# Softmax attention on one Trainium2 core: the maxima's low parts, the projections' low halves and the output sums moved to in front of a quarter's fourth maximum

## The chip, the cores and the metric

The kernel runs on one core of a Trainium2 chip. The metric is the time of one execution on the device, in microseconds (us), taken as the median of several runs. Profiled executions give a trace of each engine: TensorE (PE, matrix products), VectorE (DVE), ScalarE (ACT), GpSimd (POOL), SyncE (SP, which issues DMAs). PEld is TensorE's loading of weights.

## The reference

Two blocks are computed one after the other: a layer norm, an attention, a mixture of eight experts, and a gated sum onto the input. Only the attention of the first block is touched by the change. It is an ordinary softmax attention over 8 sequences of 512 tokens, 128 features, 16 heads of 8 features:

```python
qkv = x @ w_qkv + b_qkv
q, k, v = ...                       # (8 sequences, 16 heads, 512 tokens, 8)
attn = jnp.einsum('bhqd,bhkd->bhqk', q, k) * hd ** (-0.5)
attn = jax.nn.softmax(attn, axis=-1)
out = jnp.einsum('bhqk,bhkd->bhqd', attn, v)
return out @ w_proj + b_proj
```

## The kernel before

Each engine has its own list of instructions, written out by hand in one function per engine (`attend`), and the engines wait for one another by semaphores. An engine works through its list in order.

**Steps and quarters.** The attention runs in steps u. Step u belongs to sequence b = u // 4 and to its group of four heads g = u % 4, so that 32 steps carry exponentials; a few steps before and after fill and drain the pipeline. Each step has four quarters t, and each quarter four heads j; i = 4t + j counts from 0 to 15. The i-th turn of step u does two products on TensorE: one of scores turned around (keys by queries, L1022, semaphore `st_mm`) for step u, whose exponentials ScalarE writes (L1297, `exp_set`), and one of scores (L1028, `s_mm`) for step u + 2, whose negated row maxima VectorE takes (L1667, `max_set`). The first kind is here called an exponential's product, the second a maximum's product, S0 to S15, and its maximum M0 to M15. The maxima are added into the product of the exponentials' scores two steps later, as two more rows of the queries: a high part and a low part.

**Banks.** There are eight banks of PSUM. The maxima's products use three banks in turn (0, 1, 7), the exponentials' products three others (2, 3, 4), the output products bank 5. So a product must wait until the one three places before it has been read; the function `read_before` holds these numbers, with one exception, the sixteenth product of a step, which takes the second bank.

**Bank 6.** Everything else goes through bank 6, one small job after another:

- end of quarter 0, every step: the transpose of the step's sixteen maxima (L1052, `nmT_mm`). ScalarE copies its high part (`m_hi`, L1315), VectorE subtracts for the low part (`m_lo`, L1682, `mlo_set`), and SyncE copies both into the queries' rows.
- end of quarter 1: the transposes of the output products (L1066, `oT_mm`), which wait for `mlo_set`. VectorE then takes reciprocals of the sums of exponentials (`rden`, L1691) and normalizes (L1693), behind M7.
- end of quarter 2 and of quarter 3 in steps with g = 2: the projections of keys and of queries for the sequence after next (`project`, L324 to L326). ScalarE writes their high halves, VectorE the low halves (`low_half`, L1656, `lo_set`). The second projection waits for the low half of the first, and the next step's transpose of the maxima (g = 3) waits for the low half of the second.
- end of quarter 3 in steps with g = 0: the product with the output weights (L1099, `out_mm`). VectorE adds the bias and writes the sequence's rows (L1698, `attn_set`). The next step's transpose of the maxima (g = 1) waits for `attn_set`.

**The third place of each quarter.** Within a quarter TensorE issues the output product of the quarter before (`output`, L1123, four wide products and their weights) behind turn j = 2. So the fourth product of each quarter comes about a microsecond behind the third.

**Before the change** VectorE does the second low half behind M0 (g = 3), the low part of the maxima behind M4, the first low half behind M12 (g = 2), and the output sums behind M15 (g = 0).

Of the kernel before, what the change touches and what calls it, by code (L numbers as in the profile page):

```python
# [21 lines left out]
F32 = mybir.dt.float32  # L22
# [4 lines left out]
ALU = mybir.AluOpType  # L27
# [3 lines left out]
P = 128  # L31
# [3 lines left out]
QT = SEQ // P  # L35
# [11 lines left out]
def build(nc, x, w_qkv, b_qkv, w_proj, b_proj, router_w, w1, v1, w2, ffn_bias,  # L47
          Wq, Wk, Wv, Wc, Ltri, Wr, br, Wi, bi, Wg, bg, Wo, bo, gamma, beta, out):
    D = x.shape[2]
# [19 lines left out]
    with ctx:  # L69
        def sb(name, shape, dt=F32):  # L70
            return ctx.enter_context(nc.sbuf_tensor(name, shape, dt))

        def sem(name):
            return ctx.enter_context(nc.semaphore(name))

        ps = ctx.enter_context(nc.psum_tensor("ps", [P, 8, 512], F32))
# [5 lines left out]
        attn = sb("attn", [P, TOK_TILES, D])  # L82
# [21 lines left out]
        bproj_bc = sb("bproj_bc", [P, D])  # L104
# [56 lines left out]
        m_hi = sb("m_hi", [16, 2, P], F32R)  # L161
        m_lo = sb("m_lo", [16, 2, P], F32R)
# [12 lines left out]
        def stage():  # L175
# [116 lines left out]
        s_mm, max_set, nmT_mm, mhi_set, mlo_set, m_in = (  # L292
            sem("s_mm"), sem("max_set"), sem("nmT_mm"), sem("mhi_set"), sem("mlo_set"), sem("m_in"))
# [6 lines left out]
        onT_mm, onT_set, out_mm, attn_set = sem("onT_mm"), sem("onT_set"), sem("out_mm"), sem("attn_set")  # L300
# [9 lines left out]
        def spread(ap, axis, shape):  # L310

            return ap.unsqueeze(axis).to_broadcast(shape)
# [5 lines left out]
        def rows_of(tile, b):  # L318

            return tile[:, b * QT:(b + 1) * QT, :] if isinstance(b, int) else tile[:, bass.ds(b * QT, QT), :]  # L320
# [64 lines left out]
        def bank_of(i):  # L385


            return 1 if i == 15 else i % 3
# [5 lines left out]
        def max_head(j):  # L394

            return (j + 2) % 4
# [1079 lines left out]
        def _(dve):  # L1476
# [119 lines left out]
            def choices_between(t, j):  # L1596

                if (t, j) == (0, 0):
                    sums(0)
                if (t, j) == (0, 3):  # L1600
                    first_candidates(0)
                    choice(0)
                if (t, j) == (1, 1):
                    first_out(0)
                if (t, j) == (1, 3):
                    second_candidates()
                if (t, j) == (2, 2):
                    choice(1)
                if (t, j) == (3, 1):
                    choice_weights(0)  # L1610

            def first_tiles():

                E3 = [P, EXPERTS, EXPERTS]
                link(dve.tensor_tensor(cmp8[:, :, :], spread(off[:, :], 2, E3), spread(thr[:, :], 1, E3), ALU.is_gt))
                link(dve.tensor_reduce(ntile[:, :], cmp8[:, :, :], AX, ALU.add))
                link(dve.tensor_tensor(cmp8[:, :, :], before8[:, :, :], spread(ntile[:, :], 1, E3), ALU.mult))
                link(dve.tensor_reduce(first[:, :], cmp8[:, :, :], AX, ALU.add))
                link(dve.tensor_scalar(off[:, :], first[:, :], float(TILE), None, ALU.mult))

            def tile_experts():

                N3 = [1, TILES, EXPERTS - 1]
                link(dve.tensor_tensor(ecmp[:, :, :], spread(first[0:1, 1:EXPERTS], 1, N3),
                                       spread(tile_no[:, :], 2, N3), ALU.is_le))
                return dve.tensor_reduce(eidf[:, :], ecmp[:, :, :], AX, ALU.add)
# [27 lines left out]
            def low_half(b, o, bank):  # L1654
                dve.wait_ge(hi_set, b * 2 + (o + 1))
                dve.scalar_tensor_tensor(Lo[:, 1 - o, :], ps[:, bank, :], cols[:, 1 - o:2 - o],  # L1656
                                         Hi[:, 1 - o, :].bitcast(F32), ALU.add, ALU.subtract).then_inc(lo_set, 1)

            def attend(u, g, b, now):
                gt, v = (g + 3) % GROUPS, u + 2  # L1660
                for t in range(4):
                    for j in range(4):
                        i = t * 4 + j
                        if now.max:
                            dve.wait_ge(s_mm, v * 16 + (i + 1))
                            at = max_head(j) * 4 + t
                            dve.tensor_reduce(nmax[:, g % 2, at:at + 1], ps[:, (0, 1, 7)[bank_of(i)], :], AX, ALU.max,  # L1667
                                              negate=True).then_inc(max_set, 1)
                        if isinstance(u, int) and u == -2:
                            choices_between(t, j)  # L1670
                        if isinstance(u, int) and u == -1 and (t, j) == (2, 1):
                            dve.wait_ge(e_set[0], 2)
                            first_tiles()
                            tile_experts().then_inc(hot_set[0], 1)
                        if (t, j) == (1, 0) and now.low:

                            dve.wait_ge(mhi_set, u + 2)
                            dve.wait_ge(nmT_mm, u + 2)
                            if not (isinstance(u, int) and u + 1 < 2):
                                dve.wait_ge(m_in, u * 32)  # L1680
                            r = (g + 1) % 2
                            dve.tensor_tensor(m_lo[:, r, :], ps[0:16, 6, 0:P], m_hi[:, r, :].bitcast(F32),  # L1682
                                              ALU.subtract).then_inc(mlo_set, 1)
                        if (t, j) == (0, 0) and now.halves:
                            low_half(b + 2, 1, 6)
                        if (t, j) == (3, 0) and now.next:
                            low_half(b + 2, 0, 6)
                        if (t, j) == (1, 3) and now.tail:
                            dve.wait_ge(oT_mm, u)
                            turned = ps[:, 6, :].rearrange("p (q j r) -> p q j r", q=QT, j=4)  # L1690
                            dve.reciprocal(rden[:, :, :], turned[:, :, :, HD]).then_inc(rden_set, 1)  # L1691
                            dve.wait_ge(rden_set, u)
                            dve.tensor_tensor(onorm[:, :, 32 * gt:32 * gt + 32].rearrange("p q (j r) -> p q j r", j=4),  # L1693
                                              turned[:, :, :, 0:HD], spread(rden[:, :, :], 3, [P, QT, 4, HD]),
                                              ALU.mult).then_inc(onorm_set, 1)
                        if (t, j) == (3, 3) and g == 0 and now.tail:
                            dve.wait_ge(out_mm, b)
                            dve.tensor_tensor(rows_of(attn, b - 1), ps[:, 6, :].rearrange("p (q d) -> p q d", q=QT),  # L1698
                                              spread(bproj_bc[:, :], 1, [P, QT, D]), ALU.add).then_inc(attn_set, 1)
# [221 lines left out]
            link(dve.tensor_scalar(fbias_bc[:, :], fbias_bc[:, :], 0.5, None, ALU.mult))  # L1921
            dve.sem_inc(attn_set, 1)
            steps(dve, attend)
            experts(0)
            block1_weights()
# [29 lines left out]
```

## Time and profile before

| | us |
|---|---|
| median of 3 runs | 1088.25 |
| fastest and slowest of them | 1087.11, 1091.65 |
| span of the profiled execution | 1101.2 |

| engine | busy in the span, us | share |
|---|---|---|
| TensorE | 980.5 | 89% |
| VectorE | 852.7 | 77% |
| ScalarE | 620.6 | 56% |
| GpSimd | 572.2 | 52% |

The trace begins with the first instruction and ends with the last, so the profiled execution's own time is its span. Matrix products are pipelined and the ends of their records are modelled: a busy TensorE is not TensorE at its peak. In the rows, a number in square brackets at the end is the time the engine sat idle before the instruction, with what ended it. A gap of a few hundredths is not shown. Steps can be told apart on VectorE by the low part of the maxima (L1682), one in each step: the one at 201.74 us is that of step 9 (g = 1), 212.88 of step 10, 225.97 of step 11, 249.32 of step 13.

### The profile page before, as it was taken

How to read it: one execution, taken by the hardware profiler on the slowest of the kernel's cores; microseconds unless marked ns; L12 is line 12 of the kernel's file. 1: busy time of each engine (PE TensorE's matmuls, PEld its weight loads, DVE VectorE, ACT ScalarE, POOL GpSimd, SP SyncE). 2: the span in 40 equal slices, each digit the busy share in tenths (PEclk: the TensorE clock that was granted, in tenths of full speed). 3: DMA queues.
4: the chain of work that ended last, by engine and by line, in shares of the span. 5: the costliest groups of instructions: out<-in, count | busy, mean ns of one | idle time of the engine just before them, and what ended most of it. 6: DMA issues, size and time to landing. Idle time of an engine off the chain costs nothing. (4 is left out here: it accounts for less than half of the span.)

```text
span 1101.2 us, 18065 instructions
## 1 busy us (share of the span) xinstructions
PE 980.5 (89%) x5608; PEld 634.8 (58%) x5608; DVE 852.7 (77%) x1910; ACT 620.6 (56%) x1248; POOL 572.2 (52%) x631
## 2 busy tenths in 40 slices
PE   5789999999999999989999964999996999999960
PEld 4542344343434344368888853756655888888850
DVE  7556899999979999435555548699992899999975
ACT  6115788888868888843333326333333666777642
POOL 7220687443435442015555556378782576777770
PEclk9995999999979999999999985699997999999985
DMA  6736566353535532216666635034312677687719
GB/s 209 300 104 193 160 193 209 101 169 113 170 101 170 178 116 88 87 58 195 207 197 187 205 95 146 20 108 126 93 44 82 180 214 208 208 224 220 218 56 236
DMA packets 121521, 170.37 MB, mean 155 GB/s; under 512 B 18801, under 2 KB 80594, under 8 KB 118354
## 3 DMA queue, kind: packets, MB, share of 16 engines
q1 hardware_dynamic: 94290, 110.94, 35.1%
q0 software_dynamic: 18688, 54.08, 14.3%
q10 hardware_dynamic: 8448, 4.20, 1.5%
q8 instruction: 45, 0.74, 0.3%
q14 instruction: 50, 0.41, 0.1%
HBM read 106.71 MB, written 63.76 MB: 155 GB/s over the span
## 5 line engine op out<-in xcount | busy, mean ns | idle before, releaser
L1667 DVE TENSOR_REDUCE nmax<-ps 128x1 f32<-128x512 f32 x512 | 324.8, 683 | 50.2 <-PE ps L1028 45.6
L1297 ACT ACTIVATE stage<-ps 128x512 f32<-128x512 f32 x512 | 274.4, 594 | 75.6 <-PE ps L1022 69.6
L841 POOL DMA_INDIRECT token_y<-stage,ids_now x184 | 182.7, 993 | 130.0 <-DVE stage L1723 58.3
L1028 PE MATMUL ps<-stage,stage 32*128 32x512 f32 x512 | 189.1, 521 | 14.1 <-DVE nmax L1667 12.8
L1022 PE MATMUL ps<-stage,stage 32*128 32x512 f32 x512 | 172.3, 496 | 9.0 <-ACT stage L1297 7.5
L797 POOL DMA_INDIRECT slots_x<-xn,pos x128 | 154.5, 1207 | 40.7 <-issue 39.6
L1168 PEld LDWEIGHTS ps<-stage,stage 128*128 128x128 f32 (+1 forms) x1288 | 164.9, 191 | 13.5 <-issue 1.8
L1168 PE MATMUL ps<-stage,stage 128*128 128x128 f32 (+1 forms) x1288 | 170.9, 275 | 1.5 <-issue 1.2
L1022 PEld LDWEIGHTS ps<-stage,stage 32*128 32x128 f32 x512 | 70.3, 188 | 158.0 <-ACT stage L1297 125.9
L324 PE MATMUL ps<-stage,stage 128*128 128x512 f32 x322 | 141.1, 438 | 3.6 <-issue 3.6
L1123 PE MATMUL ps<-stage,stage 128*32 128x512 f32 x1024 | 144.2, 637 | 0.0
L326 PE MATMUL ps<-stage,stage 128*128 128x512 f32 x322 | 127.8, 397 | 0.0
L325 PE MATMUL ps<-stage,stage 128*128 128x512 f32 x322 | 127.1, 395 | 0.0
L1350 ACT ACTIVATE stage<-ps 128x512 f32<-128x512 f32 (+1 forms) x69 | 41.2, 597 | 104.8 <-PE ps L326 83.0
L1028 PEld LDWEIGHTS ps<-stage,stage 32*128 32x128 f32 x512 | 75.6, 194 | 37.7 <-DVE nmax L1667 30.2
L1787 DVE TENSOR_TENSOR stage<-ps,stage 128x512 f32<-128x512 f32 (+1 forms) x69 | 47.5, 689 | 61.6 <-PE ps L326 36.9
L1352 ACT ACTIVATE stage<-ps,ebcol 128x512 f32<-128x512 f32 x92 | 63.2, 687 | 52.8 <-PE ps L326 24.1
L1791 DVE SCALAR_TENSOR_TENSOR stage<-stage,stage 128x512 f32<-128x512 f32 x92 | 71.3, 774 | 23.3 <-ACT stage L1355 16.9
L326 PEld LDWEIGHTS ps<-stage,stage 128*128 128x128 f32 x322 | 59.8, 186 | 15.6
L324 PEld LDWEIGHTS ps<-stage,stage 128*128 128x128 f32 x322 | 60.4, 188 | 11.9 <-issue 2.3
L325 PEld LDWEIGHTS ps<-stage,stage 128*128 128x128 f32 x322 | 60.4, 187 | 8.2
L1355 ACT ACTIVATE stage<-ps,ebcol 128x512 f32<-128x512 f32 x92 | 63.2, 687 | 0.6 <-PE ps L326 0.6
(226 smaller groups left out, 1537.4 us busy)
## 6 DMA issues: line engine op xcount, KB each, us to landing
stage<-halves_w SPq DMA_DIRECT2D x23, 1024.0 KB
stage<-halves_w SPq DMA_DIRECT2D x23, 704.0 KB
stage<-slots_x SPq DMA_DIRECT2D x46, 260.0 KB
stage<-q_halves SPq DMA_DIRECT2D x32, 256.0 KB
halves_w<-stage POOLq DMA_DIRECT2D x16, 512.0 KB
k_halves<-stage SPq DMA_DIRECT2D x24, 256.0 KB
q_halves<-stage SPq DMA_DIRECT2D x24, 256.0 KB
stage<-k_halves SPq DMA_DIRECT2D x128, 48.0 KB
```

The source lines that it names most:

```text
L324: pe.matmul(out_ap, w_hi_ap, x_hi_ap, start=start, stop=False)
L325: pe.matmul(out_ap, w_hi_ap, x_lo_ap, start=False, stop=False)
L326: return pe.matmul(out_ap, w_lo_ap, x_hi_ap, start=False, stop=stop)
L797: pool.indirect_dma_start(out=slots_x[L], out_offset=bass.IndirectOffsetOnAxis(ap=pos[:, c:c + 1], axis=0), in_=xn[:, t, :], in_offset=Non ...
L841: pool.indirect_dma_start(out=token_y, out_offset=bass.IndirectOffsetOnAxis(ap=ids_now[:, r, q:q + 1], axis=0), in_=ysb[:, r, q, :], in_of ...
L1022: pe.matmul(ps[:, 2 + bank_of(i), :], head_rows(Ks, g, j)[:, t * P:(t + 1) * P], head_rows(Qs, g, j), start=True, stop=True).then_inc(st_m ...
L1028: pe.matmul(ps[:, (0, 1, 7)[bank_of(i)], :], head_rows(Qs, g2, j2)[:, t * P:(t + 1) * P], head_rows(Ks, g2, j2), start=True, stop=True).th ...
L1123: mm = pe.matmul(ps[32 * j:32 * j + 32, 5, :], vaug[:, even, t, 4 * g + j, :], probs[:, t % 2, j, :], start=(t == 0), stop=(t == 3))
L1168: mm = pe.matmul(ps[:, 5 + r, q * P:(q + 1) * P], hT[0:M, par, q * P:(q + 1) * P], wdn[0:M, r, f, :], start=(f == 0 and q == 0), stop=(f = ...
L1297: act.activation(probs[:, t % 2, j, :], ps[:, 2 + bank_of(i), :], ACT.Exp, scale=SCALE).then_inc(exp_set, 1)
L1667: dve.tensor_reduce(nmax[:, g % 2, at:at + 1], ps[:, (0, 1, 7)[bank_of(i)], :], AX, ALU.max, negate=True).then_inc(max_set, 1)
L1791: dve.scalar_tensor_tensor(hT[:, par, :], gsig[:, par, :], 1.0, gact[:, par, :], ALU.add, ALU.mult).then_inc(h_set[L], 1)
```

## The change

Four instructions of VectorE's list move. No instruction is added, removed or altered, and the lists of the other engines stay as they are, with all their waits. The second low half moves from behind M0 to in front of M3, the low part of the maxima from behind M4 to in front of M7, the first low half from behind M12 to in front of M15, and the output sums from behind M15 to in front of M3 of the next step (those of the last sequence stay where they are).

```diff
                 for t in range(4):
                     for j in range(4):
                         i = t * 4 + j
+                        if (t, j) == (0, 3) and now.halves:
+                            low_half(b + 2, 1, 6)
+                        if (t, j) == (0, 3) and g == 1 and u > 1:
+                            dve.wait_ge(out_mm, b)
+                            dve.tensor_tensor(rows_of(attn, b - 1), ps[:, 6, :].rearrange("p (q d) -> p q d", q=QT),
+                                              spread(bproj_bc[:, :], 1, [P, QT, D]), ALU.add).then_inc(attn_set, 1)
+                        if (t, j) == (1, 3) and now.low:
+                            dve.wait_ge(mhi_set, u + 2)
+                            dve.wait_ge(nmT_mm, u + 2)
...
+                            dve.tensor_tensor(m_lo[:, r, :], ps[0:16, 6, 0:P], m_hi[:, r, :].bitcast(F32),
+                                              ALU.subtract).then_inc(mlo_set, 1)
+                        if (t, j) == (3, 3) and now.next:
+                            low_half(b + 2, 0, 6)
                         if now.max:
                             dve.wait_ge(s_mm, v * 16 + (i + 1))
...
-                        if (t, j) == (1, 0) and now.low:
...
-                        if (t, j) == (0, 0) and now.halves:
-                            low_half(b + 2, 1, 6)
-                        if (t, j) == (3, 0) and now.next:
-                            low_half(b + 2, 0, 6)
...
-                        if (t, j) == (3, 3) and g == 0 and now.tail:
+                        if (t, j) == (3, 3) and u == 32:
                             dve.wait_ge(out_mm, b)
```

VectorE's list before, from the normalizing of a step with g = 2 to that of the next one; the low halves write `stage_10`, the normalizing writes `stage_4`, and `nmax` takes the maxima:

```order
L1693 TENSOR_TENSOR stage_4<-ps,rden 128x4x32
L1667 TENSOR_REDUCE nmax<-ps 128x1 x5
L1656 SCALAR_TENSOR_TENSOR stage_10<-ps,cols,stage_9 128x512
L1667 TENSOR_REDUCE nmax<-ps 128x1 x4
L1656 SCALAR_TENSOR_TENSOR stage_10<-ps,cols,stage_9 128x512
L1667 TENSOR_REDUCE nmax<-ps 128x1 x4
L1682 TENSOR_TENSOR m_lo<-ps,m_hi 16x128
L1667 TENSOR_REDUCE nmax<-ps 128x1 x3
L1691 RECIPROCAL rden<-ps 128x16
```

The same place in VectorE's list after the change (line numbers are those of the changed kernel):

```order
L1698 TENSOR_TENSOR stage_4<-ps,rden 128x4x32
L1685 TENSOR_REDUCE nmax<-ps 128x1 x7
L1656 SCALAR_TENSOR_TENSOR stage_10<-ps,cols,stage_9 128x512
L1685 TENSOR_REDUCE nmax<-ps 128x1 x4
L1656 SCALAR_TENSOR_TENSOR stage_10<-ps,cols,stage_9 128x512
L1685 TENSOR_REDUCE nmax<-ps 128x1 x4
L1678 TENSOR_TENSOR m_lo<-ps,m_hi 16x128
L1685 TENSOR_REDUCE nmax<-ps 128x1
L1696 RECIPROCAL rden<-ps 128x16
```

Seven maxima now precede the first low half (M8 to M14), and only one stands between the low part of the maxima and the reciprocals.

VectorE's list before, around the end of a step with g = 0, where `attn` takes the output sums:

```order
L1693 TENSOR_TENSOR stage_4<-ps,rden 128x4x32
L1667 TENSOR_REDUCE nmax<-ps 128x1 x8
L1698 TENSOR_TENSOR attn<-ps,bproj_bc 128x512
L1667 TENSOR_REDUCE nmax<-ps 128x1 x5
L1682 TENSOR_TENSOR m_lo<-ps,m_hi 16x128
```

The same place after:

```order
L1698 TENSOR_TENSOR stage_4<-ps,rden 128x4x32
L1685 TENSOR_REDUCE nmax<-ps 128x1 x11
L1669 TENSOR_TENSOR attn<-ps,bproj_bc 128x512
L1685 TENSOR_REDUCE nmax<-ps 128x1 x4
L1678 TENSOR_TENSOR m_lo<-ps,m_hi 16x128
```

Three maxima of the next step now precede the output sums.

TensorE's list around the same place of steps 2 and 3 mod 4, which is the same in both kernels: the second projection (L324 to L326), three turns, the output product (L1123), the fourth turn, and the transpose of the maxima (L1052). What each waits for stands behind it:

```order
L1028 MATMUL ps<-stage_12,stage_13 128x512 [waits max_set]
L324 MATMUL ps<-xT_hi,wq_hi 128x512 [waits lo_set]
...
L1123 MATMUL ps<-stage_1,stage_11 32x512 [waits exp_set]
L1123 MATMUL ps<-stage_1,stage_11 32x512 x3
L1022 MATMUL ps<-stage_13,stage_12 128x512 [waits exp_set]
L1028 MATMUL ps<-stage_12,stage_13 128x512 [waits max_set]
L1052 MATMUL ps<-ident,nmax 16x128 [waits lo_set,max_set]
L1022 MATMUL ps<-stage_13,stage_12 128x512 [waits exp_set]
```

Nothing moved there; the instruction that ends two of these waits (`lo_set`) did.

## Rows read from the trace of the kernel before

**Rows 1.** The page's costliest group: busy us, mean ns, idle before, what ended it.

```profile
L1667 DVE TENSOR_REDUCE nmax<-ps 128x1 f32<-128x512 f32 x512 | 324.8, 683 | 50.2 <-PE ps L1028 45.6
```

**Rows 2.** Windows: length, busy per engine PE PEld DVE ACT POOL, clock, DMA.

```profile
220.00:240.00 20.00, 19.46 (x124) 8.18 (x123) 18.31 (x34) 16.29 (x33) 6.79 (x10) 1.00 0.59 181
```

**Rows 3.** VectorE's timeline, steps 9 to 11: start, length, line, count, idle before.

```profile
201.74 0.27 DVE L1682 TENSOR_TENSOR m_lo<-ps,m_hi 16x128 fp32r<-16x128 f32 x1
...
203.88 0.25 DVE L1691 RECIPROCAL rden<-ps 128x16 f32<-128x16 f32 x1
...
218.44 0.69 DVE L1667 TENSOR_REDUCE nmax<-ps 128x1 f32<-128x512 f32 x1 [0.48 <-PE ps L1028]
219.04 0.74 DVE L1656 SCALAR_TENSOR_TENSOR stage<-ps,cols,stage 128x512 fp32r<-128x512 f32 x1
219.70 1.96 DVE L1667 TENSOR_REDUCE nmax<-ps 128x1 f32<-128x512 f32 x3
222.32 0.69 DVE L1667 TENSOR_REDUCE nmax<-ps 128x1 f32<-128x512 f32 x1 [0.66 <-PE ps L1028]
222.93 0.74 DVE L1656 SCALAR_TENSOR_TENSOR stage<-ps,cols,stage 128x512 fp32r<-128x512 f32 x1
223.59 2.48 DVE L1667 TENSOR_REDUCE nmax<-ps 128x1 f32<-128x512 f32 x4
225.97 0.27 DVE L1682 TENSOR_TENSOR m_lo<-ps,m_hi 16x128 fp32r<-16x128 f32 x1
...
228.12 0.25 DVE L1691 RECIPROCAL rden<-ps 128x16 f32<-128x16 f32 x1
```

**Rows 4.** TensorE's timeline, steps 9 to 11.

```profile
203.13 0.66 PE L1066 MATMUL ps<-ident,stage 128*128 128x128 f32 x4
...
220.44 0.50 PE L1028 MATMUL ps<-stage,stage 32*128 32x512 f32 x1 [0.25 <-DVE nmax L1667]
220.86 0.50 PE L324 MATMUL ps<-xT_hi,wq_hi 128*128 128x512 f32 x1
...
221.76 0.49 PE L1028 MATMUL ps<-stage,stage 32*128 32x512 f32 x1
...
223.84 0.28 PE L1052 MATMUL ps<-ident,nmax 128*16 128x128 f32 x1
224.04 0.50 PE L1022 MATMUL ps<-stage,stage 32*128 32x512 f32 x1
```

**Rows 5.** VectorE's timeline, end of step 12 and first half of step 13.

```profile
245.73 0.69 DVE L1698 TENSOR_TENSOR attn<-ps,bproj_bc 128x512 f32<-128x512 f32 x1 [0.40 <-PE ps L1099]
246.34 3.07 DVE L1667 TENSOR_REDUCE nmax<-ps 128x1 f32<-128x512 f32 x5
249.32 0.27 DVE L1682 TENSOR_TENSOR m_lo<-ps,m_hi 16x128 fp32r<-16x128 f32 x1
...
251.46 0.25 DVE L1691 RECIPROCAL rden<-ps 128x16 f32<-128x16 f32 x1
```

**Rows 6.** TensorE's timeline, first quarter of step 13.

```profile
245.62 0.49 PE L1028 MATMUL ps<-stage,stage 32*128 32x512 f32 x1
...
247.70 0.28 PE L1052 MATMUL ps<-ident,nmax 128*16 128x128 f32 x1
```

**Rows 7.** ScalarE's timeline, step 11, the exponential of turn 7.

```profile
227.48 0.60 ACT L1297 ACTIVATE stage<-ps 128x512 f32<-128x512 f32 x1 [0.88 <-PE ps L1022]
```

**Rows 8.** A window at low clock; timelines of VectorE and TensorE around it.

```profile
310.00:320.00 10.00, 10.00 (x47) 3.26 (x39) 6.01 (x12) 4.95 (x10) 3.25 (x5) 0.58 0.22 80
...
296.87 0.27 DVE L1682 TENSOR_TENSOR m_lo<-ps,m_hi 16x128 fp32r<-16x128 f32 x1
...
304.63 0.68 PE L1022 MATMUL ps<-stage,stage 32*128 32x512 f32 x1 [0.67 <-ACT stage L1297]
...
308.21 0.69 DVE L1667 TENSOR_REDUCE nmax<-ps 128x1 f32<-128x512 f32 x1 [1.34 <-PE ps L1028]
...
326.67 0.27 DVE L1682 TENSOR_TENSOR m_lo<-ps,m_hi 16x128 fp32r<-16x128 f32 x1
```

More of the change, by code:

```diff
@@ L1663, in attend @@
                         i = t * 4 + j
+                        if (t, j) == (0, 3) and now.halves:
[7 more added lines that the diff above has]
+                            dve.wait_ge(nmT_mm, u + 2)
+                            if not (isinstance(u, int) and u + 1 < 2):
+                                dve.wait_ge(m_in, u * 32)
+                            r = (g + 1) % 2
+                            dve.tensor_tensor(m_lo[:, r, :], ps[0:16, 6, 0:P], m_hi[:, r, :].bitcast(F32),
+                                              ALU.subtract).then_inc(mlo_set, 1)
+                        if (t, j) == (3, 3) and now.next:
+                            low_half(b + 2, 0, 6)
                         if now.max:
@@ L1674, in attend @@
                             tile_experts().then_inc(hot_set[0], 1)
-                        if (t, j) == (1, 0) and now.low:
[L1677 to L1683, printed above, removed]
-                        if (t, j) == (0, 0) and now.halves:
-                            low_half(b + 2, 1, 6)
-                        if (t, j) == (3, 0) and now.next:
-                            low_half(b + 2, 0, 6)
                         if (t, j) == (1, 3) and now.tail:
```

## The prediction

> **What bounds the kernel now.** I read the groups on the page first [rows 1]. The 512 maxima (L1667) are the costliest group: 683 ns each, 324.8 us in all. The windows of the attention stage come next [rows 2]: from 220 to 240 us VectorE is busy 18.31 of 20 us, TensorE is shown busy 19.46 and ScalarE 16.29, at full clock. The three work in a ring: TensorE writes a score product, VectorE takes its maximum or ScalarE its exponential, and that frees the bank for the product three places on. So I do not cost by busy shares, I follow the ring. The timelines of VectorE [rows 3, 5] and TensorE [rows 4, 6] show it. Four maxima back to back take 2.48 us [rows 3], so one follows another after (2.48 - 0.68) / 3 = 0.60 us. VectorE's gaps are short and stand where TensorE has just done a block of other work. Every step therefore has this test: does the moved instruction fill such a gap, or does it make TensorE wait for what it used to have already?
>
> The stage repeats with a period of four steps. From the low part of the maxima in step 9 (201.74 us) to that in step 11 (225.97) is 24.23 us [rows 3]. I write M0 to M15 for a step's maxima, S0 to S15 for the products that feed them. S(i) needs M(i-3), except that S15 needs M13.
>
> **No instruction is added or removed.** Cost: nothing in busy time. The whole effect is in waits on bank 6, which carries one small job after another on TensorE, each waiting for the reader of the one before. TensorE takes its list in order: in [rows 4] S15 waits until 220.44 for M13, and the projection behind it, which needs nothing of M13, goes only at 220.86. So a job of bank 6 that waits also holds every product behind it.
>
> **Low half, fourth quarter (steps 2 mod 4).** Before: M12 218.44, low half 219.04 to 219.78, M13 219.70 [rows 3]; S15 waits for M13, the projection goes at 220.86 and S0 of the next step at 221.76, M0 at 222.32 [rows 3, 4]. After: M13 at 219.04, M14 at 219.64, low half at 220.25, done 0.74 later at 220.99. S15 no longer waits, but the projection does, for the low half: with the 0.06 us that a release takes here (M13 ends at 219.70 + 0.68 = 220.38, S15 starts at 220.44 [rows 3, 4]) it goes at 221.05. That is +0.19 us, in place of the wait of 0.25 us that goes. The gap before M15 is filled and the next wait is later by more.
>
> **Low half, first quarter (steps 3 mod 4).** Before: it starts at 222.93, straight behind M0, and is done at 223.67; the maxima's transpose, which waits for it, goes at 223.84, with S4 0.2 us behind it [rows 3, 4]. After, counted from M0 at the shifted 222.51: M1 223.11, M2 223.71, low half 224.31 to 225.05, transpose at 225.11, S4 0.2 later at 225.31 and, at about 0.5 us for a product with its drain and 0.06 for the release, M4 at 225.87. M3 runs meanwhile, from 224.97. Before, M4 started at 223.59 + 3 x 0.60 = 225.39 [rows 3]. So TensorE's transpose is late by 1.27 and VectorE by 0.48, since 0.8 of it were slack.
>
> **Low part of the maxima, every step.** Before, it starts at 201.74 (step 9) and TensorE's transposes of the output sums, which wait for it, go at 203.13 with time to spare [rows 3, 4]. After, two maxima later: 201.74 + 1.20 = 202.94, done at 203.21, the transposes at 203.27, +0.14. They take 0.66 [rows 4], so the reciprocal that waits for them starts at 202.94 + 0.27 + 0.06 + 0.66 + 0.06 = 203.99 against 203.88 [rows 3]: +0.11. In a step that is already late the same chain of 1.05 us from the start of the low part is the binding one. In step 11: M4 at 225.87, low part at 227.67, reciprocal at 228.72, against 228.12 [rows 3]: +0.60, and +0.63 on TensorE, 0.19 of it from the quarter before. The steps with nothing else get +0.15.
>
> **Output sums (moved from the end of steps 0 mod 4 to the next step).** Before: 0.40 us idle, then 245.73 to 246.42, M0 at 246.34, M4 four maxima later at 248.74, the maxima's transpose at 247.70, low part 249.32, reciprocal 251.46 [rows 5, 6]. After: the idle time is longer, not shorter, as M0 must wait for S0, which starts at 245.62 [rows 6] and so lets M0 go at 246.18. Then M1 246.78, M2 247.38, output sums 247.98 to 248.67, transpose 248.73 (+1.03), S4 248.93, M4 249.49 (+0.75), low part 251.29, its chain of 1.05 to the reciprocal at 252.34: +0.88. I take 0.90.
>
> ScalarE does not bind in any of these: its high part of the maxima is late with the transpose, but four exponentials on it sits idle for 0.88 us [rows 7], which covers the 0.5 that VectorE is late. SyncE's copy of the maxima's rows starts 1.2 us later; TensorE wants them only with the next step, about 6 us on, and no row of TensorE names a DMA: nothing. While the clock is low VectorE waits 1.34 us before the fourth maximum anyway [rows 8], which hides what now stands there: nothing. In the steps before the first exponentials one low half of each kind moves too; nothing in the rows prices them but the two terms above, so I bound them by 0.19 and 0.44 on either side and take 0. From M15 of step 29 on there are no maxima and nothing moves.
>
> **The sum.** At full clock: fourth quarter 6 x 0.19 = 1.1; first quarter 6 x 0.44 = 2.6 (0.63 less the 0.19 counted); output sums 7 x 0.90 = 6.3; plain low parts 13 x 0.15 = 2.0. Together 12.0 us. The bounds: each TensorE wait in full (1.27, 1.03, 0.19, 0.14) adds up to 7.6 + 7.2 + 1.1 + 1.8 = 18, and if VectorE alone counted and later gaps took it back, 0. I take 12, since all three engines shift by about the same and the later gaps (0.48 before M12, for one) are TensorE's work standing in front, so they shift too. The profiled execution, with 1101.2 us, is 1.2% above the median of 1088.25; the stage's pattern in it is regular, so I add the 12 to the median: 1100.3 us, and to the span: 1113.
>
> **Rivals.**
> A. *The waits don't bind and the gaps are filled (faster).* Each moved instruction stands where VectorE waits for the product behind TensorE's output product. If TensorE came to its transposes later than VectorE is through, the gain would be the gap of 0.66 before M0 [rows 3] six times and the 0.40 before the output sums [rows 5] seven times: 4.0 + 2.8 = 6.8, giving 1081.5. It decides itself at one point: the transpose must come over 1.27 us later than now, behind the low half. The rows put TensorE there before that [rows 4, 6]. Chance 0.09.
> B. *The lateness is taken back.* The gaps of VectorE that these rows show, 0.48, 0.66 and 0.40 [rows 3, 5], make 1.5 us in a period, against the 1.8 that a period loses (0.19 + 0.44 + 0.90 + 2 x 0.15). If they are slack rather than TensorE's own work, the time stays within 3 us of 1088. For: a wait that I place may fall on time that the ring had free through ScalarE. Against: S12's gap stands behind a projection that is shifted too. Chance 0.15.
> C. *The clock (slower still).* Once in the steady stage the granted clock fell, after 304.6 us, and was 0.58 in the window from 310 to 320, a mix of its two levels, 1.2 and 2.4 GHz [rows 8]. What stood before was no long pause: TensorE's last one was 0.67 us. From step 17's low part (296.87) to step 19's (326.67) took 29.80 us in place of 24.23, so a fall costs 5.6 us. The change adds a pause of about 1 us to two steps in four, so one to three more falls are possible: 1106 to 1117. Against it speaks the window from 220 to 240 us, which kept the full clock through waits of its own [rows 2]. The Trainium skill has a rule for this, in "TensorE: Matmul & The Clock Gate", section "A second HAM failure mode: psum-queue depth-cycling": short idle stretches between groups of matmuls, frequent enough, make the clock go back and forth between its levels. By that rule the forecast would be this rival's; the trace agrees that the clock falls without a long pause, and shows one such fall in the stage at its regular pace. Chance 0.14.
> That the change does not do what it says is ruled out by the rows of the instruction order.
>
> **How the numbers follow.** The forecast has 0.62 (1094 to 1106, partial losses included), A 0.09, B 0.15, C 0.14. A measurement here can tell 0.5%, or 5.4 us. Slower by more: 0.62 + 0.14 = 0.76; within: 0.15; faster: 0.09. For the range I leave out A, a little of B and the upper end of C: 1088 to 1112.
>
> **What would show it.** In the changed kernel VectorE's rows should show M1 and M2 directly behind M0, then the low half or the output sums; the maxima's transpose (L1052) should be released by that instruction, about 1 us after TensorE is ready, and a new wait of TensorE's weight loads on VectorE should stand in the list of waits, some 13 times. The distance of two low parts over four steps should grow from 47.6 (201.74 to 249.32 [rows 3, 5]) to about 49.5 us, most of it in steps 1 mod 4. The reciprocal should now wait for TensorE by some 0.1 to 0.3 us in each step. I am wrong if the transpose starts without waiting (then A), if the waits are there but four steps still take 47.6 us (B), or if the windows show more stretches at half clock (C).

## The result and the profile after

| | before | after |
|---|---|---|
| median, us | 1089.71 (4 runs) | 1102.71 (4 runs) |
| fastest and slowest | 1087.11, 1091.65 | 1099.72, 1111.10 |
| span of the profiled execution | 1101.2 | 1099.4 |

The changed kernel is slower: the ratio is 1.0136, with a 95% interval from 1.0095 to 1.0176, which is 10 to 19 us. The two medians are 13.0 us apart, where the prediction said 12.0. The two spans say the opposite, and a reader who compares only these goes wrong. The profiled execution of before contains two stretches at half clock in the attention stage that the one of after does not have (from about 86 to 110 us, and the one of [rows 8]). The one of after has one that before lacks, from 24 to 80 us, which costs little: its first low part of the maxima starts at 64.86 us, before at 64.16. The change must therefore be read where both run the steps at full clock.

The maxima cost the same as in [rows 1], which was to be expected, as no instruction changed. This is the same line of the page for the changed kernel:

```profile
L1685 DVE TENSOR_REDUCE nmax<-ps 128x1 f32<-128x512 f32 x512 | 323.5, 683 | 48.6 <-PE ps L1028 40.8
```

The clean measure is the distance between two low parts of the maxima. There is one in each step, and four steps make a period. At full clock a period took 47.57 us before (47.58, 47.56 and 47.56 in three undisturbed ones) and 49.42 after (49.40 to 49.46 in five). From step 3 to step 29 the trace of before has 312.56 us, of which 5.57 belong to the fall of the clock, and the trace of after has 318.56: a difference of 318.56 - (312.56 - 5.57) = 11.6 us at full clock. This stretch holds only five of the six pairs of low halves. With the sixth, from step 2 on, it is (440.54 - 108.20) - (443.20 - 117.57 - 5.57) = 12.3 us, and this is the number to hold against the 12.0. By step:

| from the low part in a step to that in the next | before | after | difference |
|---|---|---|---|
| g = 2 to g = 3 | 13.08 | 13.79 | +0.71 |
| g = 3 to g = 0 | 11.52 | 11.60 | +0.08 |
| g = 0 to g = 1 | 11.83 | 12.79 | +0.96 |
| g = 1 to g = 2 | 11.13 | 11.25 | +0.12 |

VectorE's timeline after, in the fourth quarter of a step with g = 2 and the first half of the next (start, length, line, count, idle before); it answers to [rows 3]:

```profile
211.49 1.89 DVE L1685 TENSOR_REDUCE nmax<-ps 128x1 f32<-128x512 f32 x3 [0.45 <-PE ps L1028]
213.29 0.74 DVE L1656 SCALAR_TENSOR_TENSOR stage<-ps,cols,stage 128x512 fp32r<-128x512 f32 x1
213.95 0.68 DVE L1685 TENSOR_REDUCE nmax<-ps 128x1 f32<-128x512 f32 x1
215.55 1.89 DVE L1685 TENSOR_REDUCE nmax<-ps 128x1 f32<-128x512 f32 x3 [0.92 <-PE ps L1028]
217.35 0.74 DVE L1656 SCALAR_TENSOR_TENSOR stage<-ps,cols,stage 128x512 fp32r<-128x512 f32 x1
218.01 0.68 DVE L1685 TENSOR_REDUCE nmax<-ps 128x1 f32<-128x512 f32 x1
219.01 1.89 DVE L1685 TENSOR_REDUCE nmax<-ps 128x1 f32<-128x512 f32 x3 [0.32 <-PE ps L1028]
220.82 0.27 DVE L1678 TENSOR_TENSOR m_lo<-ps,m_hi 16x128 fp32r<-16x128 f32 x1
221.01 0.67 DVE L1685 TENSOR_REDUCE nmax<-ps 128x1 f32<-128x512 f32 x1
221.85 0.26 DVE L1696 RECIPROCAL rden<-ps 128x16 f32<-128x16 f32 x1 [0.17 <-PE ps L1066]
```

The maximum behind each low half (at 213.95, at 218.01) starts without a wait: those two gaps are indeed filled. But new gaps stand elsewhere. Before M0 it is 0.92 us in place of 0.66, before M4 there is one of 0.32 that was not there, and the reciprocal now waits 0.17.

TensorE's timeline of the same stretch shows where they come from; it answers to [rows 4]:

```profile
214.09 0.51 PE L324 MATMUL ps<-xT_hi,wq_hi 128*128 128x512 f32 x1 [0.76 <-ACT stage L1297]
...
216.65 0.50 PE L1028 MATMUL ps<-stage,stage 32*128 32x512 f32 x1
218.24 0.27 PE L1052 MATMUL ps<-ident,nmax 128*16 128x128 f32 x1 [1.10 <-DVE stage L1656]
218.44 0.50 PE L1022 MATMUL ps<-stage,stage 32*128 32x512 f32 x1
...
221.19 0.63 PE L1066 MATMUL ps<-ident,stage 128*128 128x128 f32 x4 [0.52 <-issue]
```

The transpose of the maxima (218.24) waits 1.10 us and starts 0.15 us after the low half ends (217.35 + 0.74 = 218.09). The next turn (218.44) stands behind it. The second projection (214.09) starts 0.06 us after its low half (213.29 + 0.74 = 214.03); the row names ScalarE, which had long been done, so the low half is the releaser (in four other periods the list of waits names it). The transposes of the output products (221.19) start 0.10 us after the low part of the maxima ends (221.09). Their row names no releaser, but they start 0.10 us behind it in every step from 1 to 28 of this trace, where before, at full clock, they started about 1.1 us behind it. So they now wait for the low part, which used to be ready in time.

The place of the output sums, VectorE first, then TensorE; it answers to [rows 5, 6]:

```profile
240.02 1.89 DVE L1685 TENSOR_REDUCE nmax<-ps 128x1 f32<-128x512 f32 x3 [0.84 <-PE ps L1028]
241.82 0.68 DVE L1669 TENSOR_TENSOR attn<-ps,bproj_bc 128x512 f32<-128x512 f32 x1
242.42 0.68 DVE L1685 TENSOR_REDUCE nmax<-ps 128x1 f32<-128x512 f32 x1
243.42 1.89 DVE L1685 TENSOR_REDUCE nmax<-ps 128x1 f32<-128x512 f32 x3 [0.32 <-PE ps L1028]
```

```profile
242.65 0.27 PE L1052 MATMUL ps<-ident,nmax 128*16 128x128 f32 x1 [1.04 <-DVE attn L1669]
```

The gap that the output sums used to stand in has grown from 0.40 to 0.84 us, and the transpose waits 1.04 us for them. The list of waits of the changed kernel, from 120 to 450 us (engine and line, what it waited for, us in all, times, longest), sums these up; the first two have no counterpart before, the third was 0.7 us, twice:

```profile
PE ps L1052 <- DVE stage L1656: 5.5, 5, 1.1
PE ps L1052 <- DVE attn L1669: 5.2, 5, 1.0
...
DVE rden L1696 <- PE ps L1066: 2.5, 13, 0.5
```

The reciprocal was expected to wait 0.1 to 0.3 us in each step. It waits 0.17 us in the steps 1 and 3 mod 4 (those with a low half or output sums in their first quarter); in the two others its rows show no wait.

### The profile page after: what moved, and what is told of

It reads as the page before. It is cut to its first block and busy times, and to the rows that moved or that the text cites. A ratio compares the mean times of both kernels' runs of the same rounds, so it can differ in the third digit from the quotient of the medians.

```text
span 1099.4 us, 18063 instructions
## 1 busy us (share of the span) xinstructions
PE 951.1 (87%) x5606; PEld 621.6 (57%) x5608; DVE 854.8 (78%) x1910; ACT 621.0 (56%) x1248; POOL 568.4 (52%) x631
## 5 line engine op out<-in xcount | busy, mean ns | idle before, releaser
L1028 PE MATMUL ps<-stage,stage 32*128 32x512 f32 x512 | 174.8, 500 | 8.9 <-DVE nmax L1685 8.9
L1022 PE MATMUL ps<-stage,stage 32*128 32x512 f32 x512 | 163.0, 478 | 8.8 <-ACT stage L1297 7.1
L1022 PEld LDWEIGHTS ps<-stage,stage 32*128 32x128 f32 x512 | 65.3, 182 | 149.3 <-ACT stage L1297 123.3
L324 PE MATMUL ps<-stage,stage 128*128 128x512 f32 x322 | 140.9, 438 | 3.6 <-issue 3.6
L1123 PE MATMUL ps<-stage,stage 128*32 128x512 f32 x1024 | 136.4, 605 | 0.0
L326 PE MATMUL ps<-stage,stage 128*128 128x512 f32 x322 | 127.5, 396 | 0.0
L1028 PEld LDWEIGHTS ps<-stage,stage 32*128 32x128 f32 x512 | 70.1, 188 | 23.5 <-DVE nmax L1685 16.2
L1796 DVE SCALAR_TENSOR_TENSOR stage<-stage,stage 128x512 f32<-128x512 f32 x92 | 66.5, 723 | 20.5 <-ACT stage L1355 13.8
L326 PEld LDWEIGHTS ps<-stage,stage 128*128 128x128 f32 x322 | 59.6, 185 | 15.6
L324 PEld LDWEIGHTS ps<-stage,stage 128*128 128x128 f32 x322 | 60.4, 187 | 11.9 <-issue 2.3
```

The source lines that it names most:

```text
L324: pe.matmul(out_ap, w_hi_ap, x_hi_ap, start=start, stop=False)
L326: return pe.matmul(out_ap, w_lo_ap, x_hi_ap, start=False, stop=stop)
L1022: pe.matmul(ps[:, 2 + bank_of(i), :], head_rows(Ks, g, j)[:, t * P:(t + 1) * P], head_rows(Qs, g, j), start=True, stop=True).then_inc(st_m ...
L1028: pe.matmul(ps[:, (0, 1, 7)[bank_of(i)], :], head_rows(Qs, g2, j2)[:, t * P:(t + 1) * P], head_rows(Ks, g2, j2), start=True, stop=True).th ...
L1123: mm = pe.matmul(ps[32 * j:32 * j + 32, 5, :], vaug[:, even, t, 4 * g + j, :], probs[:, t % 2, j, :], start=(t == 0), stop=(t == 3))
L1796: dve.scalar_tensor_tensor(hT[:, par, :], gsig[:, par, :], 1.0, gact[:, par, :], ALU.add, ALU.mult).then_inc(h_set[L], 1)
```

## The experiments

Each kernel ran on the chip beside the kernel before. "Period" is the distance of two low parts over four steps, taken where the clock was full. In most kernels it repeats within 0.05 us and in all within about 0.15, apart from a few periods with a single longer wait in them (47.72 to 47.76 in four overlapping periods of before). Whole executions of one kernel differ by 10 us and more, so the periods carry the comparisons and the ratios stand beside them. The theory: TensorE's jobs in bank 6 wait for the moved instruction, and every later product waits behind them. The main rival: VectorE's later gaps take the lateness back. In the diffs, lines with a plus stand ahead of the turn's maximum, as in the change, unless said otherwise.

**1. Both low halves alone.**

```diff
-                        if (t, j) == (0, 0) and now.halves:
+                        if (t, j) == (0, 3) and now.halves:
-                        if (t, j) == (3, 0) and now.next:
+                        if (t, j) == (3, 3) and now.next:
```

> Only the two low halves move (behind M2 in steps 3 mod 4, behind M14 in steps 2 mod 4); output sums and low part of the maxima stay. Measure: the distance of two low parts of the maxima over four steps at full clock, 47.58 us before, 49.44 after. My theory (TensorE's jobs of bank 6 wait for the moved instruction): the first quarter's transpose waits about 1.1 us, the second projection 0.2, and with the low part of the maxima in its old place VectorE loses the 0.48 by which M4 is late: 48.0 to 48.1, in all +3 us. Rival (VectorE's later gaps take it back): 47.6, in all 0.

Measured: period 48.00 (+0.43), ratio 1.0086 (1.0050 to 1.0122). The period is the theory's. The ratio (9.4 us, at least 5.4) is clearly more than the period explains (6 x 0.43 = 2.6 us). In the profiled execution the clock fell once in the stage (below), which cost 58.5 - 48.0 = 10.5 us; that falls like it make up the rest in the timed runs is likely, but no trace of them shows it.

**2. The output sums alone.**

```diff
+                        if (t, j) == (0, 3) and g == 1 and u > 1:
-                        if (t, j) == (3, 3) and g == 0 and now.tail:
+                        if (t, j) == (3, 3) and u == 32:
```

> Only the output sums move, from behind M15 to in front of M3 of the next step. My theory: the transpose of the maxima in steps 1 mod 4 waits about 1 us for them, M4 is 0.75 us late; four steps 48.3 (+0.75), in all +5 us. Rival (absorbed): 47.6. If the cost were only the 0.40 us gap that the old place filled, 48.0, in all +3.

Measured: period 48.28 (+0.71), ratio 1.0042 (1.0000 to 1.0083). TensorE's transpose in this kernel:

```profile
243.24 0.27 PE L1052 MATMUL ps<-ident,nmax 128*16 128x128 f32 x1 [1.04 <-DVE attn L1666]
```

The wait is there without any other part of the change, and the cost is above the 0.40 of the lost place.

**3. The low part of the maxima alone.**

```diff
-                        if (t, j) == (1, 0) and now.low:
+                        if (t, j) == (1, 3) and now.low:
```

> Only the low part of the maxima moves, from behind M4 to in front of M7. My theory: the transposes of the output sums start 0.14 us later in each step and the reciprocal waits for them; four steps 48.0 to 48.1 (+0.5), in all +3 to +4 us. Rival (the gap in front of M7 is filled and nothing is late): 47.5, in all -1.

Measured: period 47.95 (+0.38), ratio 1.0047 (1.0004 to 1.0090). Slower, a little less than expected: 0.09 us a step.

The three parts alone add up to 0.43 + 0.71 + 0.38 = 1.52 us, all together cost 1.85. The distances by step show where the other 0.33 stands. With the low halves alone the low part of step 3 mod 4 is 0.59 us late (13.67 in place of 13.08), but the next distance is 0.17 shorter than before (11.35 for 11.52). With the output sums alone it is 0.88 late (12.71 for 11.83) and the next one 0.16 shorter (10.97 for 11.13). So 0.33 us of a period are taken back there. In the changed kernel nothing is: its distances behind these steps (11.60 and 11.25) are those of the low part alone (11.58 and 11.24). That it is the chain from the low part of the maxima over the transposes to the reciprocal which forbids it, as the prediction has it, agrees with the 0.17 us that the reciprocal waits in just these steps; no run isolates the chain.

**4. One maximum further (dose).** The output sums in front of M4 instead of M3.

```diff
-                        if (t, j) == (0, 3) and g == 1 and u > 1:
+                        if (t, j) == (1, 0) and g == 1 and u > 1:
```

> As the run with the output sums alone, but one maximum later still: in front of M4 instead of M3. My theory: nothing is left that VectorE could do while the transpose and S4 follow, so the whole 0.60 us of a further maximum is added: four steps 48.9 (+1.35), in all +9 us against before. Rival (only the lost fill of the gap counts, wherever the sums stand): the same as with the output sums in front of M3.

Measured: period 48.89 in the undisturbed one (+1.32 against before, +0.61 against the output sums in front of M3). One maximum, 0.60 us, is added in full, as the theory has it, and the transpose waits 1.64 us in place of 1.04. TensorE and VectorE there:

```profile
198.20 0.27 PE L1052 MATMUL ps<-ident,nmax 128*16 128x128 f32 x1 [1.64 <-DVE attn L1666]
```

```profile
197.37 0.68 DVE L1666 TENSOR_TENSOR attn<-ps,bproj_bc 128x512 f32<-128x512 f32 x1
198.97 0.69 DVE L1671 TENSOR_REDUCE nmax<-ps 128x1 f32<-128x512 f32 x1 [0.91 <-PE ps L1028]
```

The four timed runs took 1112 to 1184 us, too far apart for a ratio and far more than the 9 us of the periods. The one that was profiled (1131.65 us) had the clock fall six times in steps 1 to 28 (below); the others have no trace.

**5. The wait taken away, the moves kept.** TensorE's transpose of the maxima goes behind turn 5 instead of turn 3, and ScalarE's high part with it, in steps 1 to 28. All of the change stays on VectorE. (`turn_maxima` is the block that stood at the end of quarter 0, with its waits.)

```diff
+                        if (t, j) == (1, 1) and 1 <= u <= 28:
+                            turn_maxima()
-                    if t == 0 and now.low:
+                    if t == 0 and now.low and not 1 <= u <= 28:
...
-                        if (t, j) == (0, 3) and now.low:
+                        if (t, j) == ((1, 1) if 1 <= u <= 28 else (0, 3)) and now.low:
```

> The changed kernel, with TensorE's transpose of the maxima behind turn 5 instead of turn 3, and ScalarE's high part behind the exponential of turn 5, in steps 1 to 28: S4 and S5 no longer stand behind the wait for the moved instruction. My theory: the transpose's wait was the larger part of the cost; what stays is the gap that the output sums no longer fill (0.4), the second projection (0.2) and the chain of the low part (0.1 to 0.15 a step): four steps 48.4 to 48.7 in place of 49.44. Rival (the order on VectorE itself costs, not TensorE's wait): 49.4.

**6. The same late transpose with low halves and output sums in their old places**, low part of the maxima in front of M7.

> The same late transpose, but low halves and output sums in their old places (low part of the maxima in front of M7). My theory: 48.0 to 48.1 for four steps, as with the low part alone moved, since the late transpose costs nothing. The difference to the run with all moved is what the moved instructions cost when no transpose waits for them: 0.4 to 0.6. Rival: if the late transpose has a cost of its own, this run is slower than the one with the low part alone, by that.

Measured: period 48.54 with all moved, 47.94 with the old places; ratios 1.0039 (1.0008 to 1.0070) and 1.0017 (0.9980 to 1.0054). The second equals the period of the low part alone (47.95), so the late transpose has no cost of its own. With it the transpose waits only briefly in the kernel with all moved:

```profile
202.21 0.27 PE L1016 MATMUL ps<-ident,nmax 128*16 128x128 f32 x1 [0.20 <-DVE attn L1671]
```

Of the 1.85 us of a period, 49.42 - 48.54 = 0.88 were TensorE's wait at the transpose. Of the other 0.97, the low part accounts for 0.37 (47.94 against 47.57), and 0.60 are what low halves and output sums cost when the transpose hardly waits. By step these are 13.38 - 13.21 = 0.17, which fits the second projection, and 12.37 - 11.93 = 0.44, which fits the gap in front of step 1 mod 4 that stays empty. The rival that only the order on VectorE costs is refuted, since that order is the same with the early and the late transpose.

**7. The first low half one maximum later, the rest as before.**

```diff
-                        if (t, j) == (3, 0) and now.next:
+                        if (t, j) == (3, 1) and now.next:
```

> The kernel before with one move in the other sense: the first low half behind M13 instead of behind M12 (steps 2 mod 4). My theory: S15 no longer waits 0.25 us for M13, and the second projection, which needs the low half, goes about 0.4 us earlier (220.44 in place of 220.86 on the rows' clock): four steps 47.2 (-0.4), in all -2.5 us (0.2%). Rival (the old place was already the best, since the low half is ready only then): 47.6.

Measured: period 47.13 (-0.44). (The line stays behind the turn's maximum.) S15 no longer waits for M13. The low half ends later than in its old place, and the projection waits 0.17 us for it, but the projection goes 208.18 - 206.18 = 2.00 us behind the start of M12, in place of 220.86 - 218.44 = 2.42 [rows 3, 4]. VectorE, then TensorE:

```profile
206.18 1.29 DVE L1667 TENSOR_REDUCE nmax<-ps 128x1 f32<-128x512 f32 x2 [0.47 <-PE ps L1028]
207.38 0.74 DVE L1656 SCALAR_TENSOR_TENSOR stage<-ps,cols,stage 128x512 fp32r<-128x512 f32 x1
```

```profile
207.52 0.49 PE L1028 MATMUL ps<-stage,stage 32*128 32x512 f32 x1
208.18 0.50 PE L324 MATMUL ps<-xT_hi,wq_hi 128*128 128x512 f32 x1 [0.17 <-DVE stage L1656]
```

So the same instruction gains 0.44 behind M13 and loses 0.18 behind M14 (9, below), where the projection goes 210.08 - 207.48 = 2.60 us behind M12. As 6 x 0.44 = 2.6 us are 0.24%, the whole execution does not show it: 0.9988 (0.9946 to 1.0030), and in the second set of runs

> The kernel before with the first low half behind M13 alone, beside the one with the two products: period 47.13 us, median within 1085 to 1090.

1.0008 (0.9974 to 1.0041), with the period at 47.14.

**8. The second low half alone.**

> Only the second low half moves, from behind M0 to in front of M3 in steps 3 mod 4. My theory, worked out as in the prediction without the shift from the quarter before: transpose at 224.92 in place of 223.84, M4 late by 0.29 us; four steps 47.85. Rival: 47.58.

Measured: period 47.80 (+0.23), ratio 1.0043 (1.0011 to 1.0075).

**9. The first low half alone.**

> Only the first low half moves, from behind M12 to in front of M15 in steps 2 mod 4. My theory: the second projection waits for it and goes 0.19 us later; four steps 47.77. Rival (the wait of S15 that goes outweighs it): 47.3 to 47.5.

Measured: period 47.75 (+0.18), ratio 1.0002 (0.9971 to 1.0033). The two together make 0.41, and both in one kernel 0.43: they add.

**10. The changed kernel again.**

> The changed kernel once more, beside the others on one chip. Expected: four steps 49.44, about 1.2% slower than before.

Measured: 1109.03 us against 1090.51 for the kernel before in the same set of runs, ratio 1.0152 (1.0091 to 1.0214), period 49.43. The period repeats to 0.01 us, and the kernel is slower again. The medians are 18.5 us apart this time, 6 more than the periods explain; in the profiled execution the clock fell once in the steps, which cost about 5.5 us.

**11. Two products in TensorE's pause.** The traces so far raised a second question: where does the clock fall? In the 13 profiles of before, of after and of the runs above it fell twelve times in steps 1 to 28. Six times it was right behind the same kind of place, a wait of about 0.67 us before turn 1 (five times in steps 2 mod 4, once in step 27), as here, in the kernel with the two low halves moved (TensorE; the output product that follows takes 1.94 us instead of 1.07):

```profile
200.73 0.59 PE L1022 MATMUL ps<-stage,stage 32*128 32x512 f32 x1 [0.67 <-ACT stage L1297]
...
201.49 1.94 PE L1123 MATMUL ps<-stage,stage 128*32 128x512 f32 x8
```

Four times it was behind the 1.64 us wait of experiment 4, and twice, in experiment 6, there was no wait over 0.25 us just ahead. There are nine waits of 0.67 us in each profile, 117 in all, so a fall behind one of them is rare. Outside these steps the clock fell too: in step 0, from about 85 us, in three profiles, and behind step 28 in several. The kernel of 7 got two products that nobody reads, in that place:

```diff
+                        if (t, j) == (0, 1) and g == 2 and 1 <= u <= 28:
+                            pe.wait_ge(onorm_set, u - 1)
+                            for _ in range(2):
+                                pe.matmul(ps[:, 6, :], wq_hi[:, 0, :], xT_hi[:, 0, :], start=True, stop=True)
```

> The kernel with the first low half behind M13, and two products of 512 columns into bank 6, whose result nobody reads, in front of turn 1 of steps 2 mod 4. There TensorE waits 0.67 us for ScalarE in each period, and in the traces of before, and of the run with both low halves moved, the granted clock fell right behind that wait. If that pause decides on the clock: the period stays at 47.13 us, steps 1 to 28 show no fall in the profile, and the slow upper half of the timed runs goes (median 1084 to 1086). If the clock falls for another reason: the same spread as without, median about 1088. If the two products are too long for the pause: a longer period.

Measured: 1082.22 us, ratio 0.9965 (0.9938 to 0.9993): slightly faster than the kernel before, and by more than expected. The period is 47.12, so the products fit into the pause:

```profile
197.44 0.73 PE L1019 MATMUL ps<-xT_hi,wq_hi 128*128 128x512 f32 x2
198.18 0.50 PE L1026 MATMUL ps<-stage,stage 32*128 32x512 f32 x1
```

What changed is how the runs are spread. Of its 12 runs, 10 took 1080.5 to 1086.0 us and two 1092 to 1093; of the 24 runs of the kernel without the two products, 6 took less than 1086.0 (2 of the 12 in the same set of runs). The windows of its profile show the full clock through the stage (length, busy of the five engines, clock, DMA):

```profile
200.00:300.00 100.00, 98.77 (x646) 41.02 (x645) 93.85 (x170) 83.44 (x165) 44.05 (x53) 1.00 0.46 146
300.00:400.00 100.00, 98.10 (x643) 40.82 (x643) 93.62 (x168) 82.93 (x163) 46.22 (x52) 1.00 0.50 155
```

So do those of both profiles of 7, so the profiles do not show that the filled pause is the reason. They speak rather for another place. The two profiled executions of the kernel of 7 span 1082.0 and 1095.3 us, and neither has a fall in steps 1 to 28. Of the 13.3 us between them, 9.9 stand between the low parts of steps -1 and 3 (66.07 against 56.09 us), where in the slower one the clock fell at 85 us (its window, as above):

```profile
80.00:100.00 20.00, 18.34 (x77) 5.91 (x76) 12.01 (x20) 10.06 (x20) 2.09 (x4) 0.63 0.54 173
```

The two products first come in step 2, behind that fall, and cannot prevent it. So the timed runs show that the two products changed the times; that they did it by the pause in steps 2 mod 4 is not shown. Nor was it tried whether the pause as such decides, or the time at which these products come.

## Why the prediction was right

**The test** (does the moved instruction fill a gap or make TensorE wait) gave the right answer, and both things happened as it said: the gaps in front of the fourth maxima are filled, and the waits on bank 6 are longer by more. A period was forecast to lose 0.19 + 0.44 + 0.90 + 2 x 0.15 = 1.83 us and lost 1.85.

**Term by term.** The first low half was forecast at +0.19 and costs 0.18 alone. The second: M4 was to be 3.36 us behind M0 (0.29 more than the 3.07 of before) and is 219.01 - 215.55 = 3.46. The mis-sized piece is the release: I took 0.06 us from the low half's end to the transpose, as for a product, and it takes 0.15. Alone this part costs 0.23, where 0.27 was expected. The output sums: an empty gap of 0.85 before M0 was worked out, 0.84 measured; the wait of the transpose 1.03, measured 1.04; the step was to lose 0.90 and loses 0.96, of which 0.71 come from the sums alone. The low part: 0.15 a step forecast, 0.08 to 0.12 in the steps with nothing else, so this term was too large by a third. The chain of 1.05 us from low part to reciprocal measures 221.85 - 220.82 = 1.03. The errors are small and of both signs, which is why the sum of 12.0 meets the 12.3 between steps 2 and 29. That the two medians lie only 1 us from the forecast is in part luck: single runs of one kernel scatter by more than that whole difference, and the second set gave 18.5 us.

**What the sum left out.** The profile's own span was taken as 1101.2 and forecast to rise to 1113; it fell to 1099.4. That forecast was wrong: the span of before contained two stretches at half clock in the steps, of which the prediction discussed only one. Such stretches differ between executions of one kernel: of the two profiled executions of the kernel of experiment 7, one has the fall in step 0 and the other has not. Adding the 12 us to the median was the part that held.

**Rivals.** A (faster) named its deciding point, a transpose over 1.27 us later. Experiment 5 moved it by two turns; the wait went, and the kernel was still 0.97 us a period slower than before, so A had a second condition that I missed: the projection and the low part's chain would have had to be late as well. B (taken back) is refuted for the changed kernel, but it has something for it where the low part of the maxima stays in its old place: in experiments 1 and 2, 0.17 and 0.16 us of the lateness were taken back. C (the clock) is open. Against it, in both profiles of the changed kernel the transposes wait 1.0 to 1.1 us twice in each period and no fall followed one of these waits. For it, the second set of medians and those of experiment 1 lie further apart than the periods explain, and the one fall in the second profile of the changed kernel cost about 5.5 us. One maximum further it fell behind four of the five waits of 1.64 us, and the loss was several times that of the periods. The Trainium skill's rule in "TensorE: Matmul & The Clock Gate", section "A second HAM failure mode: psum-queue depth-cycling", that short idle stretches between groups of products can make the clock go back and forth, agrees with that run, whose clock fell and came back six times in steps 1 to 28. It does not say which stretches, and the length alone does not tell here: all 45 waits of 1.0 to 1.1 us at the transpose and the product ahead of it passed, while six of the 117 waits of 0.67 us were followed by a fall. It may have a part in the 0.7 us by which the median (13.0) exceeds the periods (12.3), and in the 6 us of the second set; the measurement is too wide to tell.

## What to carry to other kernels

An engine's idle time in front of an instruction is no free place as long as another engine waits for what you put there: list the consumer of the moved instruction, and compare the end of the move with the time at which the consumer is ready now. In an in-order list the consumer's wait also holds everything behind it, so the output sums, moved later by three maxima, cost 0.71 us a period although the gap in front of M3 was filled. The best place is the one that lets the consumer go earliest, all its waits counted. For the first low half this was not the earliest place: one maximum later than before gained 0.44 us a period, although the projection then waited 0.17 us for it, and two later lost 0.18. Compare periods inside the trace at one clock, not spans.

## What the runs showed of the hardware

The granted clock of TensorE fell to its half level (1.2 of 2.4 GHz) in a stage that shows TensorE busy 97% of the time (19.46 of 20 us, [rows 2]), behind some waits of 0.67 us (6 of 117) and most waits of 1.64 us (4 of 5), and twice without a wait over 0.25 us. Single falls cost from 2.6 us (experiment 2) to 10.5 us (experiment 1), 5.6 in the profile of before. With two products of no use, 0.73 us on TensorE, in one such wait of a period the median was 1082.22 us, against 1088.94 for the same kernel without them and 1087.44 for the kernel before in the same set of runs. I had taken the scatter of executions (1084 to 1110 us for one and the same kernel) for something the kernel cannot influence; these runs say that in part it can, though not by which way.
